# Softmax shifts of three graph attentions computed on VectorE in batches, and wide bf16 products in the spare columns of the second attention's accumulators

## The reference

```
layer 0, 1 head:   s = x_att @ neib_att.T + own;  s = leaky_relu(s, 0.01);  mask; softmax; agg = p @ value(128)
layer 1, 4 heads:  h = n @ W.T;  s[i,j] = leaky_relu(src[i] + dst[j], 0.2);  mask; softmax; out = p @ h(64 per head)
layer 2:           o = sum over k of (adj == k) @ (n @ wk) + bias            (no softmax)
layer 3:           s = leaky_relu(Wh1[i] + Wh2[j], 0.2);  p = softmax(s), q = -softmax(-s), both masked
                   out = elu(concat(p @ n, q @ n) @ wtrans)
x = x + step; then x = x + experts(layernorm(x)), 16, 8, 8 and 16 experts, the top two of each node
```

## Time and profile before

| what | value |
| --- | --- |
| three timed runs | 1139.75, 1142.49, 1142.68 us; median 1142.49 |
| the profiled execution's own time | 1139.45 us |
| its span, first to last instruction | 1137.6 us |
| mean granted TensorE clock | 0.914 |
| busy over the span: PE, DVE, ACT, POOL | 84%, 62%, 44%, 41% |
| first attention (layer 0) | 46.7 to 82 us of the span |
| second attention (layer 1) | 271.7 to 398 us |
| third attention (layer 3) | 856 to 942 us |

### The profile page before, as it was taken

How to read it: one execution, slowest core, us unless ns; L and a number is a source line. 1 busy time by engine, 2 the same in 40 slices (tenths; PEclk the granted TensorE clock), 3 DMA queues, 4 the chain that set the end, 5 groups by cost and what they waited for, 6 DMA issues and landing times. The chain is left out here.

```text
span 1137.6 us, 23844 instructions
## 1 busy us (share of the span) xinstructions
PE 956.3 (84%) x7670; PEld 901.1 (79%) x7670; DVE 710.7 (62%) x1649; ACT 500.6 (44%) x953; POOL 462.4 (41%) x490
## 2 busy tenths in 40 slices
PE   6884976876888949856998989999888994999993
PEld 4574976876888949855898989999865884999992
DVE  4785655694778657647554546656555877566664
ACT  1341665413655527631104467777524441343441
POOL 1242554234777536620132025554134532444441
PEclk8795999898988869987998999999988996999997
DMA  6006975410000054746124001119620005755853
GB/s 242 1 29 200 296 233 175 125 56 2 5 11 10 11 195 120 227 131 219 38 84 168 11 15 38 37 41 334 226 79 2 10 15 219 267 165 179 312 168 130
DMA packets 62943, 137.16 MB, mean 121 GB/s; under 512 B 10224, under 2 KB 40976, under 8 KB 58128
## 3 DMA queue, kind: packets, MB, share of 16 engines
q1 hardware_dynamic: 52640, 111.27, 28.3%
q0 software_dynamic: 9024, 24.65, 7.6%
q10 hardware_dynamic: 1200, 0.23, 0.1%
HBM read 201.90 MB, written 17.56 MB: 193 GB/s over the span
## 5 line engine op out<-in xcount | busy, mean ns | idle before, releaser
L1819 PE MATMUL r_pH<-e_xsT,e_w 128*128 128x128 f32 x2304 | 278.3, 278 | 27.2 <-DMA e_w<-w_in 23.8
L1819 PEld LDWEIGHTS r_pH<-e_xsT,e_w 128*128 128x128 f32 x2304 | 268.5, 194 | 30.9 <-issue 25.4
L1773 POOL DMA_INDIRECT y_rows<-e_ys,e_to x94 | 149.4, 1590 | 226.7 <-DVE e_idx L1918 113.4
L1930 DVE TENSOR_TENSOR e_w_lo<-e_w,e_w_hi 128x1024 fp32r<-128x1024 f32 (+1 forms) x94 | 137.9, 1467 | 41.3 <-ACT e_w_hi L1877 39.9
L1834 PE MATMUL r_pY<-e_w_hi,e_h_hi 128*128 128x256 f32 x464 | 140.6, 303 | 6.5 <-issue 4.5
L1783 POOL DMA_INDIRECT e_xs<-xn_rows,e_idx x94 | 105.7, 1124 | 96.6 <-DVE e_idx L1918 71.0
L1877 ACT ACTIVATE e_w_hi<-e_w 128x1024 fp32r<-128x1024 f32 (+1 forms) x94 | 117.1, 1246 | 60.3 <-DMA e_w<-w_in 59.2
L1834 PE MATMUL r_pY<-e_w_lo,e_h_hi 128*128 128x256 f32 x464 | 132.7, 286 | 0.0
L1834 PE MATMUL r_pY<-e_w_hi,e_h_lo 128*128 128x256 f32 x464 | 132.6, 286 | 0.0
L464 ACT ACTIVATE g_t<-g_g,g_small 128x1024 f32<-128x1024 f32 x56 | 64.2, 1152 | 108.5 <-POOL g_small L451 108.5
L1834 PEld LDWEIGHTS r_pY<-e_w_hi,e_h_hi 128*128 128x128 f32 x464 | 90.6, 195 | 7.4 <-issue 5.9
(11 more groups left out here) (317 smaller groups left out, 1851.3 us busy)
## 6 DMA issues: line engine op xcount, KB each, us to landing
e_w<-w_in SPq DMA_DIRECT2D x56, 1024.0 KB
e_w<-w_in SPq DMA_DIRECT2D x84, 512.0 KB, 8.3
e_w<-w_in SPq DMA_DIRECT2D x52, 514.0 KB
e_w<-w_in SPq DMA_DIRECT2D x24, 1028.0 KB
e_b<-b_in SPq DMA_DIRECT2D x76, 128.0 KB
e_w<-y_rows SPq DMA_DIRECT2D x32, 256.0 KB, 5.1
p_adj<-adj_in SPq DMA_DIRECT2D x8, 512.0 KB, 10.8
xn_rows<-xn SPq DMA_DIRECT2D x32, 128.0 KB, 1.7
```

What stands on the lines that cost most here:

```text
L1773: pool.indirect_dma_start(out=y_rows[:, :], in_=ys[b][:, :], in_offset=None, out_offset=bass.IndirectOffsetOnAxis(ap=to[b][:, :], axis=0))\
L1819: ins = nc.tensor.matmul(pH[b % 2][:, f, :], w1[b][:, at:at + P], xsT[b % 2][:, c, :], start=(c == 0), stop=(c == DC - 1))
L1930: nc.vector.tensor_tensor(w2_lo[b % 2][:, :], w2[b][:, :], w2_hi[b % 2][:, :].bitcast(F32), ALU.subtract).then_inc(w2_split, 1)
```

## The change

The biases move from GpSimd to VectorE, and are computed for several units at once. `batches` lists how many units each batch has; behind the mask that completes a batch VectorE waits for its own maximum and issues three small operations (in layer 3 four, since units alternate between max and min). `lead` is how many units the masks run ahead of before: 2 in layer 0, 4 in layers 1 and 3; there are `lead + 4` tiles `g`. ScalarE's slope waits for its unit's batch. In layer 0 the scores also run `lead` units further ahead. In layer 1 TensorE issues four bf16 products of `ones_b`, 4 x 63 = 252 columns wide, into the unread columns of the accumulator bank before each weigh but the first of a group. GpSimd keeps only the reciprocal roots.

```diff
         def attention(block, ph, heads, slope, lowest, rows, rest, values, width, finish,
-                      scores=None, extra=(), group=1):
+                      scores=None, extra=(), group=1, lead=4, batches=()):
             units = NT * heads
-            g = [ph.sb(f"g{n}", [P, N]) for n in range(4)]
+            G = lead + 4
+            ends = {sum(batches[:k + 1]): k for k in range(len(batches))}
+            batch_of = [k for k, size in enumerate(batches) for _ in range(size)]
+            g = [ph.sb(f"g{n}", [P, N]) for n in range(G)]
...
                 def mask(u):
-                    if u >= 4:
-                        dve.wait_ge(sloped, u - 3)
-                        dve.wait_ge(shifted, u - 3)
+                    if u >= G:
+                        dve.wait_ge(sloped, u - G + 1)
+                        dve.wait_ge(shifted, u - G + 1)
...
                         op0=ALU.add, op1=ALU.max, accum_out=gm[:, u:u + 1]).then_inc(maxed, 1)
+                    if u + 1 in ends:
+                        biases(u + 1 - batches[ends[u + 1]], u + 1)
+
+                def biases(lo, hi):
+                    c = slice(lo, hi)
+                    dve.wait_ge(maxed, hi)
+                    link(nc.vector.scalar_tensor_tensor(out=bent[:, c], in0=gm[:, c], scalar=-slope, in1=rest[:, c],
+                                                        op0=ALU.mult, op1=ALU.add))
+                    kinds = 2 if lowest(1) else 1
+                    for k in range(kinds):
+                        q = slice(lo + k, hi, kinds)
+                        ins = nc.vector.scalar_tensor_tensor(out=b1[:, q], in0=gm[:, q], scalar=-1.0, in1=bent[:, q],
+                                                             op0=ALU.mult, op1=ALU.max if lowest(k) else ALU.min)
+                    link(ins)
+                    nc.vector.tensor_tensor(b2[:, c], b1[:, c], rest[:, c], ALU.subtract).then_inc(biased, 1)
...
+                for u in range(lead):
+                    mask(u)
                 for u in range(units + 4):
-                    if u < units:
-                        mask(u)
+                    if u + lead < units:
+                        mask(u + lead)
...
             def _(pool):
                 for u in range(units):
-                    c = slice(u, u + 1)
-                    pool.wait_ge(maxed, u + 1)
-                    link(nc.gpsimd.tensor_scalar(bent[:, c], gm[:, c], -slope, rest[:, c], ALU.mult, ALU.add))
-                    link(nc.gpsimd.tensor_scalar(b1[:, c], gm[:, c], -1.0, bent[:, c], ALU.mult,
-                                                 ALU.max if lowest(u) else ALU.min))
-                    nc.gpsimd.tensor_tensor(b2[:, c], b1[:, c], rest[:, c], ALU.subtract).then_inc(biased, 1)
...
                 def slope_of(u):
-                    act.wait_ge(biased, u + 1)
+                    act.wait_ge(biased, batch_of[u] + 1)
...
                 def weigh(u):
...
+                    if part > 0:
+                        rest_of_bank = 512 // group - width
+                        for _ in range(4):
+                            nc.tensor.matmul(o[k % 2][:, :, width:], ones_b[:, :],
+                                             bc(ones_b[:, 0:rest_of_bank].unsqueeze(1), [P, group, rest_of_bank]),
+                                             start=True, stop=True)
...
 layer 0: lead=2, batches=(1, 1, 2, 2, 2)
 layer 1: lead=4, batches=(1, 1, 2) + (H,) * (NT - 1)      # H = 4
 layer 3: lead=4, batches=(2, 2, 4, 4, 4)
```

More of the change, by code:

```diff
@@ L417, in shift @@
                     nc.vector.scalar_tensor_tensor(
[L418 removed]
+                        out=lm[u % 2][:, :], in0=g[u % G][:, :], scalar=b1[:, u:u + 1], in1=t2[u % 4][:, :],
                         op0=ALU.add, op1=ALU.min if lowest(u) else ALU.max).then_inc(shifted, 1)
@@ L516, in weigh, with score @@
                     ins.then_inc(weighed, 1)
+                def score(u):
+                    if u >= 2:
+                        pe.wait_ge(maxed, u - 1)
+                    scores(u).then_inc(scored, 1)
                 if scores:
-                    for u in range(2):
-                        scores(u).then_inc(scored, 1)
+                    for u in range(2 + lead):
+                        score(u)
                 for u in range(units + 3):
-                    if scores and u + 2 < units:
-                        pe.wait_ge(maxed, u + 1)
-                        scores(u + 2).then_inc(scored, 1)
+                    if scores and u + 2 + lead < units:
+                        score(u + 2 + lead)
                     if 2 <= u < units + 2:
@@ L535, in attend @@
         def attend(block, ph, front, heads, slope, lowest, rows, rest, values, width, finish, scores, done, free=0,
-                   settle=None, more=(), group=1):
+                   settle=None, more=(), group=1, lead=4, batches=()):
             units = NT * heads
@@ L636, in attend @@
                     hooks[name] = more[name]
-            attention(block, ph, heads, slope, lowest, rows, rest, values, width, finish, scores, hooks, group)
+            attention(block, ph, heads, slope, lowest, rows, rest, values, width, finish, scores, hooks, group, lead, batches)
         def graph0(gate_of):
@@ L869, in graph0 @@
                        lambda u: S[u % 2][:, :, :].rearrange("p a b -> p (a b)"),
-                       rest, lambda u, c: V[:, c, :], OUT + 1, finish, scores, lambda t: t + 4, NT)
+                       rest, lambda u, c: V[:, c, :], OUT + 1, finish, scores, lambda t: t + 4, NT,
+                       lead=2, batches=(1, 1, 2, 2, 2))
         class BeforeGraph1(Handover):
@@ L1047, in graph1 @@
                           rest[:, :, :].rearrange("p t h -> p (t h)"),
-                          lambda u, c: V[:, c, u % H, :], DH + 1, finish, None, lambda t: (t + 1) * H + 3, group=H)
+                          lambda u, c: V[:, c, u % H, :], DH + 1, finish, None, lambda t: (t + 1) * H + 3, group=H,
+                          batches=(1, 1, 2) + (H,) * (NT - 1))
         def graph2(gate_of, own_weights):
```

10 lines of the change are left out of this document (4 added, 6 removed).

## The result

| what | before | after |
| --- | --- | --- |
| median of four runs each | 1142.59 us | 1154.84 us (1148.96 to 1156.77) |
| ratio after to before, 95% interval | | 1.0101 [1.007, 1.0133] |
| profiled execution, span | 1139.45, 1137.6 us | 1155.11, 1153.4 us |
| mean granted clock | 0.914 | 0.899 |

The forecast was 1145.9 us and at most 1154. The direction was right; the loss in this comparison is 12.3 us over the median of before instead of the 3.4 forecast. In two later comparisons on other chips, 12 runs of the changed kernel each, the medians lie 4.9 us (1157.39 against 1152.47) and 5.6 us (1147.43 against 1141.85) above the kernel before. So there is a loss, and its size varies; the experiments explain much of both.

A forecast was written before the change was run, and what follows sets the result against it. VectorE was taken to bound the first attention, GpSimd's chain the second, TensorE the third. Terms 2.9 + 0.5 + 1.4 = +4.8 us on a mean of 1141.1 gave 1145.9 us, range 1138 to 1154.

The forecast's parts named there:

- A batch, 0.7 us: VectorE: three small operations and the maximum's readout, less overlap with the next mask, cost 0.7 us; bounds 0.25 to 0.9.
- First attention, +2.9: First attention: five batches add 3.5 us on VectorE, which sets the pace; taken as +2.9 us, ends 0 and +4.5.
- Second attention, its start, +6.2 at the seventh turn: Second attention's start: more masks, batches and wide products ahead make TensorE's seventh turn 6.2 us later.
- I keep that length: Second attention's start: the half clock still lasts 9.2 us after the first turn, so it ends at 292.
- Its middle: Second attention, seventh to 27th turn: five groups of 13.95 instead of 15.4 us, a gain of 7.2 us at undisturbed clock.
- I take one fall: Second attention's middle: one fall of the clock, at +2.2 us each, putting the whole second attention at +0.5 us.
- Its end, -0.7: Second attention, 27th turn to last finish: TensorE's own work of 21.3 us instead of 22.0, a gain of 0.7 us.
- Third attention, +1.4: Third attention: second shift stands behind another mask and batch, delaying the second turn; +1.4 us, ends 0 and +3.
- Rival 2: Second attention: clock falls in nearly every group, five falls and a longer half-clocked start, +10 us more, 1156; chance 0.14.
- Rival 1: Second attention: wide products hold the clock at 1.00, no fall comes; together about -1.4 us, or -4, 1137; chance 0.15.
- Rival 3: Whole kernel: it evens out, batches at 0.4 us and the clock as forecast, +1 us, 1142; chance 0.21.
- Rival 4: Second attention: wide products hold nothing and cost 8.5 us; the rest is GpSimd's removed chain; no separate chance.

The follow-up runs named there:

- 13: Kernel before with only its second attention changed, wide products included; first and third as before: 1146.45 us, ratio 1.0034 to the kernel before.
- 16: The changed kernel itself, run again on another chip: median 1147.43 us over 12 runs, 5.6 us above the kernel before; ratio 1.0024.
- experiment 5: The changed kernel itself, run again on another chip: 1157.39 us over 12 runs, ratio 1.0057 to the kernel before.
- experiment 9: Changed kernel, finish one step later, no other products, plus 88 wide products before the second attention's first turn and 12 behind it: 1122.6 us, ratio 0.983.
- 7: Changed kernel without wide products, each tile's finish in the second attention one step later in VectorE's order: 1138.24 us, ratio 0.9879 to the kernel before.
- experiment 3: Changed kernel with eight more wide products in TensorE's hole behind each tile's first weigh, second attention: 1142.74 us, ratio 1.0008 to the kernel before.
- 4: Changed kernel with 48 wide products ahead of the second attention's first turn: 1150.31 us, ratio 1.0104 to the kernel before.
- 1: Changed kernel without its wide products, shifts and batches left as they are: 1145.18 us, ratio 1.0014 to the kernel before.
- 6: Changed kernel without wide products before the weighs, with eight in TensorE's hole behind each tile's first weigh: 1142.26 us, ratio 0.9916 to the kernel before.
- 14: Kernel before with only its second attention changed, without wide products: 1140.21 us, ratio 0.999 to the kernel before.
- experiment 8: Changed kernel with wide products only in the hole, and masks two ahead instead of four in layers 1 and 3: 1144.0 us, ratio 0.9925.
- 2: The kernel before with the wide products alone, biases still on GpSimd: 1139.95 us, ratio 0.9993 to the kernel before.

## Why the prediction was wrong

**A batch, 0.7 us.** 0.59 in layers 0 and 1, 0.65 in layer 3. Right. The Trainium skill's 58 cycles ("VectorE: DVE Perf Modes", § The TRN2 errata) would make an estimated 0.06 us; these take 0.16 in the rows and start 0.20 apart, each waiting for the one before. The trace decides, and the choice against that row of its table held. The same section of the Trainium skill goes on to say that the row gives too little for single operations, and has (N + 151) / 0.96 ns for an fp32 addition of two tensors, which at one column is an estimated 0.16 us; with that the trace agrees. The working had left this out. With GpSimd silent VectorE's masks and shifts are as long as before (medians of 1219 and 1280 ns against 1218 and 1281), so to give nothing for that was right.

**First attention, +2.9.** +1.8 in the first profile, but 3.9 to 5.0 in seven of the eleven profiles with batches, and +3.4 on average. The number is near, partly by luck: five batches are 3.0 us, and the term has nothing for the fall of the clock behind the 2.1 us wait or for the longer half clock at the start, which make up the spread.

**Second attention, its start, +6.2 at the seventh turn.** It came at 36.6 us after the first mask instead of 27.3: +9.3. The first turn was right (11.1 against 11.4 us). "I keep that length" was a step that failed, the smaller of two: the half clock lasted 16.0 us from the first turn (280.6 to 296.6) and not 9.2, so that the six turns took 25.5 us instead of 22.1. That differs between executions: the profiles of 13 and 16 have the same 16 us and a seventh turn at 36.5 us, that of experiment 5 has 10.7 us and 34.0, which is near the forecast's 33.5. TensorE had been idle for 13.4 us rather than 9.1, and the first turns stand 3 us apart; experiment 9, where it was fed, shows what is left without the long half clock (first finish 2.7 us earlier than in 7).

**Its middle.** The sum for a group, 13.95 us, was right to 0.05: 14.0 in experiments 3, 4 and 5; and 13.05 without products is 13.1 in 1 and 6. The step that failed most is "I take one fall" with "+2.2 each". The profile has five falls, and each costs 3.1 us (17.1 less 14.0): 5 x (17.1 - 15.4) = +8.5 instead of -7.2 + 2.2 = -5.0. The price was too low because the hole lies ahead of the fall and not inside it (the turn that ends the hole starts at 323.19, the clock falls at 323.90), so next to nothing of the 3.4 us is hidden. The number was wrong because I read the three falls before as rare events; they went with a hole that stands in every group, and the change left it there while it took away the slack of GpSimd's chain that made a fall cheap (0.6 us). In experiment 5 the same step fails with three falls instead of five.

**Its end, -0.7.** It came out at -1.8 (20.2 us from the 27th turn to the last finish instead of 22.0).

**Third attention, +1.4.** It came out at +0.7, in each of the ten profiles with batches and a lead of four. Its first turns:

```profile
881.76 1.09 PE L514 MATMUL g_tp<-ident,g_lm 128*128 128x128 f32 x8 [0.69 <-ACT own_own_room L1291]
884.66 1.09 PE L514 MATMUL g_tp<-ident,g_lm 128*128 128x128 f32 x8 [1.81 <-DVE g_lm L435]
```

The new wait is there, 1.81 us for the 1.5 worked out; but the first turn itself came 10.8 us after the first mask instead of 11.4, which gives back 0.7.

**Sum.** In the profile start, middle and end are +16.0 instead of +0.5; the other two are 1.8 us under their terms, and the rest of the span is 2.6 us shorter, with a first mask that came 3.9 us earlier. So the error is one step, the time at half clock: 13.5 us of it through the falls in the middle and 3.1 at the start. The later comparisons, +4.9 and +5.6 us, lie close to the forecast's sum of +4.8. That nearness is luck and no credit to the working: the profile of experiment 5 has three falls of 3.1 us and not one of 2.2, and a stage 7 us longer than before instead of 0.5.

**The rivals.** Rival 2 is what the profile shows, with its mechanism (a shorter group leaves the same hole), its five falls and its longer start: 1156, measured 1155.1. By the medians of the two later comparisons the loss is far nearer to the forecast's number than to its. Still it deserved more than 0.14. For it stood that all three falls of the earlier trace rows began right behind a hole, and that nothing in the change touches it. Rival 1's claim that the products hold the clock is refuted by experiments 5 and 13; with the products in the hole no fall came (experiment 3), though the total was then level with the kernel before and not below it. Rival 3 describes at most single executions of the changed kernel (the lowest of experiment 16 is 1136.5). Rival 4, that they hold nothing, is right in that they prevent no fall, and wrong in that they shorten it; its 8.5 us were 5 to 6 on the one chip where both kernels ran (14 against 13, medians of 1140.2 and 1146.5).

The Trainium skill ("TensorE: Matmul & The Clock Gate", § A second HAM failure mode: psum-queue depth-cycling) describes a kernel in which frequent short idles of TensorE between groups of matmuls are enough to let the clock go back and forth. The trace agrees: in the second attention waits of 1.2 us in each group were enough, though not behind every one, and waits of 0.4 to 0.6 us were not.

**What stays open.** Which hole the first fall takes: the changed kernel's stage ran through two holes at full clock in experiment 5 (through four in 4) and fell at the first in the three other profiles. The length of a wait alone doesn't tell: waits of 0.99 us in every group of experiment 8 and two of 1.3 us in the first attention of the kernel before let no fall come, 1.23 us in the second attention did. The stage begins at another moment in each execution (268.7 to 281.9 us over the profiles), and no run here fixes that moment. Also open is why the three comparisons of the changed kernel give 4.9 to 12.3 us. What its profiles differ in is of that size (two falls at 3.1 us each, 2.6 us at the start of the second attention, 2.3 in the first), but only profiled executions show it.

## What to carry to other kernels

When a stage's pace passes to TensorE, count what a fall of its clock costs there, and where it starts: a short wait that recurs in every group can let it fall in every group (the second attention as changed had five falls in three of its four profiles and three in the other). Look for that wait in the order of the other engines (here VectorE waited for a tile's last weigh ahead of the next shift; moving the finish one step back took 16 us off the stage, 126.5 to 110.9) before filling it with products, and if products must fill something, put them in the wait itself. A term that hangs on the clock gets a range of its own, with all groups falling as one end that is likely, not remote. And profile a kernel more than once before reading a stage's cost from it: here one pair of profiles gave 1.8 us for the first attention and eighteen gave 3.4.

## What the runs showed of the hardware

- The times at half clock differ between executions of one kernel: the changed kernel's three profiles have 5, 3 and 5 falls and differ by 9 us in one stage; 12 runs of it lie 24 us apart (1136.5 to 1160.8), and for runs without a profile that this is the reason isn't shown.
- A fall in the middle of the stage lasted 3.4, 6.8, 10.3 or 13.6 us, and was shorter where the wide products stood behind the hole: 3.4 instead of 6.8 us in the kernel before (2 against the earlier trace rows), always 6.8 in the changed one, which without them had 6.8 to 13.6 (1 and 14).
- A single wait of TensorE of 2.1 us in the first attention was followed by a fall of 3.4 us in 7 of 11 profiles.
- Small VectorE operations in a chain cost 0.20 us from start to start, whether 1, 2 or 4 columns wide.
- 48 products of 252 columns take 5.4 us at full clock, 0.113 us each: the estimate from 128 columns, 0.114, held. 88 take 11.4 us with 3.4 us of half clock in them.
